# A two-layer net on one core: six more spare matmuls on TensorE around the gate and the compression

## The reference

```
x = LN(x + attn0(x))          # 16 heads of 64, softmax over 256 keys
x = LN(x + ffn0(x))           # router: 8 clusters x 8 tiles; per token a small spline network
x = LN(x + attn1(x))          # linear attention and a window of 65 keys, mixed by a gate
x = LN(x + ffn1(x))           # causal attention, then a soft mixture of 8 experts
```

## Time and profile before

| | us |
|---|---|
| median of 3 runs | 2405.09 |
| lowest and highest | 2404.09, 2405.84 |
| the profiled execution | 2407.1 |
| its span, first to last instruction | 2405.3 |
| mean granted clock of TensorE in it | 0.968 |
| busy: PE, PEld | 2214.3, 1543.1 |
| busy: DVE, ACT, POOL | 1557.6, 1348.8, 848.4 |

### The profile page before, as it was taken

One profiled execution on the slowest core, in us unless ns is written; L12 is line 12 of the kernel. 1 busy time (PEld: TensorE's weight loads), 2 busy tenths in 40 slices (PEclk: granted clock), 3 DMA queues, 4 the chain that ended last, 5 costly groups with the idle time before them and its releaser, 6 DMA issues.

```text
span 2405.3 us, 44055 instructions
## 1 busy us (share of the span) xinstructions
PE 2214.3 (92%) x16144; PEld 1543.1 (64%) x16144; DVE 1557.6 (65%) x4247; ACT 1348.8 (56%) x3784; POOL 848.4 (35%) x1010
## 2 busy tenths in 40 slices
PE   7749999999999999999999999999999999998897
PEld 5536666766668566675667665676666756667465
DVE  4566686586766866677665767558675676656642
ACT  4417573665647645476554756466564764546442
POOL 2313461145510644107531256114561054510630
PEclk9869999999999999999999999999999999999899
DMA  4000001010010000100001100000001000010001
GB/s 147 27 0 1 1 1 36 19 32 1 1 45 10 31 1 1 53 31 3 1 5 50 32 1 1 27 28 32 1 1 45 10 32 1 1 44 2 31 1 49
DMA packets 24561, 50.44 MB, mean 21 GB/s; under 512 B 3284, under 2 KB 3868, under 8 KB 23964
## 3 DMA queue, kind: packets, MB, share of 16 engines
q1 hardware_dynamic: 24348, 47.62, 6.1%
HBM read 45.52 MB, written 2.10 MB: 20 GB/s over the span
## 4 chain that ended last, share of the span: by engine, by line
PE 77%; DVE 11%; ACT 5%; POOL 4%; issue 2%; DVEq 0%; ACTq 0%
PE ps L1450 10%; PE ps L1471 10%; PE ps L639 5%; PE ps L656 5%; PE ps L594 5%; PE ps L834 4%; PE ps L1388 4%; PE ps L872 4%; PE ps L1483 4%; PE ps L1405 4%; PE ps L765 3%; PE ps L748 3%; PE ps L1343 2%; PE ps L801 2%; PE ps L1354 2%; POOL rn L1693 2%
## 5 line engine op out<-in xcount | busy, mean ns | idle before, releaser
L1012 POOL TENSOR_TENSOR rstd<-ve,half_neg 128x4 f32<-128x4 f32 (+1 forms) x56 | 66.9, 1195 | 984.6 <-DVE ve L993 984.6
L1471 PEld LDWEIGHTS ps<-wbuf,QK 128*128 128x128 f32 x2048 | 265.9, 191 | 108.2 <-issue 99.9
L1266 POOL TENSOR_TENSOR E<-E,ri 128x512 f32<-128x512 f32 x240 | 247.8, 1042 | 184.3 <-DVE ri L1065 184.2
L1574 ACT ACTIVATE QK<-ps,cols 128x512 f32<-128x512 f32 x256 | 172.9, 687 | 211.1 <-PE ps L1450 210.8
L1450 PE MATMUL ps<-h2T,wbuf 128*128 128x512 f32 x512 | 277.2, 630 | 0.2
L1700 POOL TENSOR_TENSOR work<-work,ri 128x128 f32<-128x128 f32 x480 | 231.8, 508 | 120.8 <-DVE ri L1623 120.0
L1471 PE MATMUL ps<-wbuf,QK 128*128 128x128 f32 x2048 | 270.2, 275 | 0.0
L895 ACT ACTIVATE E<-ps,nm 128x256 f32<-128x256 f32 x480 | 225.5, 484 | 64.2 <-DVE nm L1058 64.0
L1534 ACT ACTIVATE work<-ps,nm 128x128 f32<-128x128 f32 x480 | 198.5, 425 | 99.4 <-DVE nm L1614 99.4
L1693 POOL TENSOR_TENSOR rn<-ss,half_neg 128x8 f32<-128x8 f32 x120 | 195.2, 1638 | 160.1 <-DVE ss L1599 159.3
L1058 DVE TENSOR_REDUCE nm<-ps 128x2 f32<-128x512 f32 x256 | 168.9, 684 | 24.1 <-PE ps L639 22.5
(11 more groups left out here) (280 smaller groups left out, 4502.8 us busy)
## 6 DMA issues: line engine op xcount, KB each, us to landing
wbuf<-in_w SPq DMA_DIRECT2D x128, 256.0 KB, 3.2
xT<-in_xT SPq DMA_DIRECT2D x8, 256.0 KB, 3.5
xr<-in_xr SPq DMA_DIRECT2D x8, 256.0 KB, 4.2
bias_t<-in_bias_t SPq DMA_DIRECT2D x1, 2048.0 KB
out_y<-xn SPq DMA_DIRECT2D x8, 256.0 KB, 2.0
wqkv<-in_wqkv SPq DMA_DIRECT2D x1, 1536.0 KB
wo<-in_wo SPq DMA_DIRECT2D x2, 512.0 KB, 9.2
rows<-in_rows SPq DMA_DIRECT2D x1, 531.0 KB, 7.2
```

The source lines that it names most:

```text
L1266: nc.gpsimd.tensor_tensor(L.E[:, g % 4, :, :], L.E[:, g % 4, :, :], L.ri[:, g, :].unsqueeze(2).broadcast_to((P, NT, S)), ALU.mult)\
L1471: last = nc.tensor.matmul(bank2[2 + x % 2][:, t * P:(t + 1) * P], hid[:, x % 2, c, t * P:(t + 1) * P], w2[:, x % WB, c, :], start=(c == 0) ...
```

## The change

Two calls of `spare_work` are added, three matmuls each. One stands in `first_pe` in front of the wait for the gelu, into `bank1[3]`, in inner parts alone; the compression's matmuls write this bank next. The other stands in `second_pe` between the transposes of the output and the wait for their copy, into `bank2[1]`, in all parts from 1 to 8; the second L1450 writes this bank next.

```
             last.then_inc(s["route_ready"], 1)
             yield
+            if both:
+                spare_work(pe, bank1[3], 3)
             pe.wait_ge(s["gelu_ready"], upto("gelu_ready", 1))
...
             pe.wait_ge(s["o2_ready"], upto("o2_ready", 1))
             transposed(bank2[2], xn2).then_inc(s["o2_tr"], 1)
+            spare_work(pe, bank2[1], 3)
             pe.wait_ge(s["o2T_ready"], upto("o2T_ready", 1))
```

## The result

| | kernel before | changed kernel |
|---|---|---|
| median of 20 runs, us | 2405.63 | 2410.89 |
| lowest, highest | 2404.09, 2415.72 | 2399.95, 2421.25 |
| profiled execution, its span | 2407.1, 2405.3 | 2406.52, 2404.7 |
| mean granted clock in it | 0.968 | 0.972 |

The ratio is 1.0017, 95% interval [1.0009, 1.0024]. 2394.3 us was forecast, 0.5% faster. The changed kernel also scatters more, and the scatter goes with the clock: of the 20 executions the one at 2399.95 had a mean granted clock of 0.975, ten between 2409.9 and 2414.4 had 0.968 to 0.970, and the two at 2421 had 0.963. Only the execution at 2406.52 left a trace of this set, so which stretch of the longer ones was at half clock is not known.

A forecast was written before the change was run, and what follows sets the result against it. TensorE's own pace bounds it (busy 92%), its clock halving once per inner part. 12.7 - 1.6 - 0.3 = 10.8 us saved; from the profiled 2407.1 us this gives 2396.3, from the median 2405.1 the forecast 2394.3; range 2389 to 2400 us.

The forecast's parts named there:

- The spares are hidden: In both filled waits: three spares take 0.69 us, leaving 0.40 and 0.33 us, so no cost at full clock.
- Theory C: Posed after the result: the spares cost time themselves, with gate to compression above 1.99 us; no chance given.
- The fall at the gate goes: Around the gate and compression matmuls: granted clock 1.00 where 0.50 stood, in at least five of seven parts.
- What it gives: Inner parts: full clock from the compression to the gate's transposes wins 2.01 us in part 1, 12.7 us over seven.
- The step that failed: From 380.10 to 383.46, called the slackest stretch left: falls return in two of seven parts, 1.6 us given back.
- (c): Behind the compression: the fall moves into dense work, 3.4 us lost in place of 1.8; 2416 us, chance 0.06.
- The prediction's own sign of being wrong: Inner parts: falls in dense stretches that had none would show the forecast wrong; no size given.
- (b): Inner parts: the fall goes in half of them, three or four meet the beat badly; 2398.7 us, chance 0.12.
- (a): At the filled waits: the spares are too little and the clock falls as before; 2407 us, chance 0.09.
- (d): At the two 0.93 us waits: idle times are harmless, filling changes nothing; 2405.1 us, chance 0.03.
- The rule of the Trainium skill: At the 0.93 us waits: drops come only of longer idle gaps between matmul bursts, so filling these brings nothing.
- The bounds of +-3 us for the last part: Last part: its other falls meet the work elsewhere; taken as zero, bounds -3 and +3 us.

The follow-up runs named there:

- The two runs with one place alone: Changed kernel with only the three spares behind the output's transposes, 2407.28 us (0.9998), or only the three before the compression's wait, 2407.77 us (1.0007).
- The run with D: Changed kernel plus five spare matmuls in front of the wait for the gate's transposed copy (`gateT_ready`); 2393.65 us, ratio 0.9945.
- the second trace: The changed kernel run again unaltered for another trace; 2405.72 us, ratio 0.9995 to the kernel before.
- three at B: Kernel before with only the three spares in front of the compression's wait for the gelu; 2407.77 us, ratio 1.0007.

## Why the prediction was wrong

- *The spares are hidden* was right: 1.59 and 1.99 us as before, at no cost where the clock is up. In the last part 0.3 us was forecast, 0.03 measured. Theory C is refuted.
- *The fall at the gate goes* was right: it is gone from 0.8 to 1.9 us behind the gate in all seven parts, and the compression runs at full clock; only in part 6 does another begin right behind the compression. The two runs with one place alone show that it takes both.
- *What it gives* was near: L1459 1.73 us sooner (1.66 forecast), L1463 1.77 us sooner (2.01 forecast). The 0.35 us at the gate's transposes did not come. VectorE took up their copy 1.07 us after L1459 began (385.53 to 386.60), and not 0.75, since it was at L1024 and L1025 just then; the wait at L1463 is 1.20 us, not 0.77 as before, and the new one at L1459 is 0.68, not 0.8 to 1.0. Measured by parts without a fall, all seven were worth 11.4 us (9.9, and, by the length of part 6, 286.74 - 285.25 = 1.5 as an estimate for the seventh), not 12.7.
- *The step that failed* is the one on what is left: "The slackest stretch left is from 380.10 to 383.46", and the term it gave, two falls of seven and 1.6 us given back. Measured were falls in six of seven parts and 10.1 us given back over the first six. I had looked only between the two places filled, and the words against (c), "four L1450 stream for 1.7 us just before", let me give the fall's move into dense work 0.06. That stretch was not the slackest. The one behind it had two waits, 0.68 and 1.20 us, and between and behind them groups of 8 columns and of 8 rows, at which the prediction did not look; rival (c) had named the two waits, and I argued it away. The run with D shows it: with this stretch filled, the falls 8 to 9 us behind the gate are gone. The prediction's own sign of being wrong, falls in dense stretches that had none, is what came.
- Rival (c) is the mechanism that came true, in six of seven parts in the second trace and five in the first. Its price was off. I had put the new fall at 6.83 us and 3.4 us of loss; four of the five in the first trace are 3.41 us long and cost 1.65 us each. So it took back the gain and little more in the two traces, where (c) said 2416. What made the median of the first set 2410.89 is not shown.
- The forecast's term for what is left fits the kernel that fills this stretch as well: with D two of seven falls returned (two were forecast) at 0.67 us each (0.8 forecast). That its time, 2393.65 us, is also the number forecast is in part luck: in the traces its first six parts are 8.5 us shorter than before, and the stretch from gate 7 to gate 8 is 6.2 us shorter (220.66 for 226.82), of which only some 1.5 can be the seventh fall; the forecast had the rest at zero.
- A slip without weight: the chances of the forecast and (b) add to 0.82, those of (a) and (d) to 0.12, not 0.81 and 0.13.
- The rule of the Trainium skill weighed in the prediction, that drops come of idle gaps ("TensorE: Matmul & The Clock Gate", "Why this matters for your kernels"), gave 2405.1 us, and the time came out near it, but not for that reason: filling gaps of 0.93 us did move the falls, and with D filled the clock fell or not by which spares stood there, with the same idle time.
- The bounds of +-3 us for the last part were too narrow: from gate 7 to gate 8 the traces show 220.65 to 228.18 us.

## What to carry to other kernels

Where TensorE's clock falls once in each round of a loop, list every thin stretch of the round, not just the one ahead of the fall: clearing the first hands the fall to the next, and here a fall half as long cost as much, because it lay in dense work (9.9 us won, 10.1 given back). A round that keeps its length though the waits in it got shorter is the sign. Fill with matmuls of all rows (those of 8 rows did not do here), and leave a margin in the wait for the case that they run at half clock. Check the time against more than one trace: where the falls lie changes between executions.

## What was not expected of the hardware

- Five bf16 matmuls of 128 rows and 8 columns of weights kept the clock at 1.00 as well as five full ones (2393.51 and 2393.65 us). Five of 8 rows and 128 columns, just as long, did not (2412.52 us, the fall back at 8.49 us behind the gate).
- The same program met the falls differently from execution to execution: 2399.95 to 2421.25 us for one kernel on one core, with mean clocks of 0.975 to 0.963, while the kernel before, whose trace has its fall at the same place in each inner part, had 18 of 20 runs between 2404.09 and 2406.74 us.
- Spares in a wait whose end falls into half clock cost: three at B in 1.37 us in place of 0.69, with the compression 0.65 us later.
